# Keys of four edge chunks computed later, clearings moved on ScalarE, first gathers five slots later

## What is computed

```python
h = relu(layernorm(x))
H = gelu(h @ W1.T + b1)                       # nodes x 128
W_tar = gelu(H[src] @ WA.T) @ WB.T             # edges x 4
agg = segment_sum(H[src][:, :, None] * W_tar[:, None, :], dst)      # nodes x 128 x 4
agg = gelu(agg)
out_edge = einsum('ehm,em->eh', agg[dst], W_tar)
agg_node = segment_sum(out_edge, dst) / max(count(dst), 1)
out = gelu(concat([agg_node, H])) @ W2.T + b2
return x + out
```

## Time and profile before

| | |
|---|---|
| median of three runs | 1301.7 us (1298.65 to 1304.33) |
| the profiled execution | 1304.83 us, its span 1303.1 us |
| PE busy | 1070.4 us (82%) |
| DVE busy | 947.6 us (73%) |
| POOL busy | 903.8 us (69%) |
| ACT busy | 604.1 us (46%) |
| mean granted clock of TensorE | 0.927 |

### The profile page before, as it was taken

How to read it: one execution, slowest core, us unless ns; L and a number is a source line. 1 busy time by engine, 2 the same in 40 slices (tenths; PEclk the granted TensorE clock), 3 DMA queues, 4 the chain that set the end, 5 groups by cost and what they waited for, 6 DMA issues and landing times.

```text
span 1303.1 us, 25372 instructions
## 1 busy us (share of the span) xinstructions
PE 1070.4 (82%) x7395; PEld 727.5 (56%) x7395; DVE 947.6 (73%) x2601; ACT 604.1 (46%) x1304; POOL 903.8 (69%) x923
## 2 busy tenths in 40 slices
PE   5665127789999989999999999899999997889558
PEld 3454013356767656666666666566666654566324
DVE  7998558888888668888678887578887763532147
ACT  6765664436666445656445655356655200000224
POOL 4766657667777777777777777777777777767037
PEclk9867559989999999999999999999999998999859
DMA  5244552226666655555655555655555567655422
GB/s 206 100 161 190 227 208 56 54 76 169 181 167 175 179 156 164 156 156 156 187 164 157 157 163 159 179 151 156 155 156 152 158 197 163 201 139 161 119 76 83
DMA packets 83891, 201.11 MB, mean 154 GB/s; under 512 B 21917, under 2 KB 33375, under 8 KB 81553
## 3 DMA queue, kind: packets, MB, share of 16 engines
q1 hardware_dynamic: 58282, 142.37, 34.9%
q0 software_dynamic: 25472, 57.11, 18.1%
HBM read 167.18 MB, written 32.22 MB: 153 GB/s over the span
## 4 chain that ended last, share of the span: by engine, by line
PE 46%; DVE 17%; POOL 14%; issue 10%; DMA 7%; ACT 5%; DVEq 2%; SPq 0%; ACTq 0%; POOLq 0%
PE ps L1398 19%; POOL q L664 12%; PE ps L1379 11%; PE ps L1351 10%; DMA q<-node_table,src_g 4%; PE ps L1354 3%; DVE big L1084 2%; PE ps L1403 2%; DVE q L1093 1%; ACT hot_b L800 1%; DVE big L1280 1%; DVE mask L1059 1%; DVE big L1015 1%; DVE big L1029 1%; DVE q L948 1%
## 5 line engine op out<-in xcount | busy, mean ns | idle before, releaser
L664 POOL DMA_INDIRECT q<-node_table,src_g x796 | 770.1, 968 | 273.2 <-issue 216.6
L1398 PE MATMUL ps<-big,q 128*128 128x298 bf16 (+2 forms) x2940 | 464.0, 297 | 0.0
L800 ACT ACTIVATE hot_b<-iota_b,q 128x128 bf16<-128x128 bf16 x847 | 269.7, 389 | 343.8 <-PE ps L1379 343.6
L1351 PE MATMUL ps<-mask,q 128*128 128x96 f32 x1592 | 254.4, 283 | 76.7 <-DVE mask L1059 75.4
L1398 PEld LDWEIGHTS ps<-big,q 128*128 128x128 bf16 x2940 | 264.7, 98 | 82.7 <-issue 2.7
L1093 DVE TENSOR_SCALAR q<-iota_a,q 128x490 bf16<-128x490 f16 (+1 forms) x847 | 269.3, 365 | 24.7 <-issue 12.5
L1379 PE MATMUL ps<-q,hot_b 128*128 128x490 bf16 (+1 forms) x847 | 233.9, 372 | 58.5 <-ACT hot_b L803 25.0
L1351 PEld LDWEIGHTS ps<-mask,q 128*128 128x128 f32 x1592 | 216.7, 194 | 112.2 <-DVE mask L1059 100.7
L1084 DVE TENSOR_TENSOR big<-big,ps 128x490 f32 (+1 forms) x358 | 232.4, 649 | 55.1 <-PE ps L1379 53.8
L1059 DVE TENSOR_TENSOR mask<-eq,q 128x192 f32<-128x192 bf16 x398 | 141.5, 356 | 124.2 <-DMA q<-node_table,src_g 97.0
L1379 PEld LDWEIGHTS ps<-q,hot_b 128*128 128x128 bf16 x847 | 69.9, 97 | 161.4 <-DVE big L1084 61.4
(11 more groups left out here) (134 smaller groups left out, 776.9 us busy)
## 6 DMA issues: line engine op xcount, KB each, us to landing
q<-product_parts SPq DMA_DIRECT2D x245, 388.0 KB
product_parts<-big SPq DMA_DIRECT2D x12, 1552.0 KB, 5.9
q<-node_table,src_g POOLq DMA_INDIRECT x796
node_table<-big SPq DMA_DIRECT2D x12, 280.0 KB, 3.1
own_part<-big SPq DMA_DIRECT2D x12, 256.0 KB, 2.9
...
```

What stands on the lines that cost most here:

```text
L664: pool.indirect_dma_start(out=ring[:, t % R, :], out_offset=None, in_=table, in_offset=bass.IndirectOffsetOnAxis(ap=src_g[:, t:t + 1], axi ...
L800: last = nc.scalar.activation(hot_b[:, b % 2, i, :], iota_b[:, :], ACT.Abs, bias=nkey_b[:, t:t + 1])
L1351: nc.tensor.matmul(o[:, 0:MIX * W], ring[:, s + t, 0:D], mask[:, b, t, :, :], start=(t == 0), stop=(t == G - 1))
L1398: last = nc.tensor.matmul(ps[:, 3 + m, 0:n], c[:, LEAD + P * (MIX * part + m):LEAD + P * (MIX * part + m + 1)], counts[k % 2][:, a, c0:c1] ...
```

## The change

Keys of chunks 5 and 4 are still computed in the prologue, in steps 6 and 7. Those of chunks 3, 0, 2 and 1 are computed by DVE in the product stages: at slots 10 and 26 of stage 1, slot 26 of stage 2 and slot 26 of stage 3. Eight slots earlier SP loads the slices of destinations, sources and tile bounds that they need (three DMAs) into the memory of `stage`. The groups of chunk 0 move to stages 2 to 4. ACT's one clear of 9800 columns becomes one of 2800 in step 9 and one of 7000 in step 15; of six wipes two go to step 7 of the prologue's loop, and the other four into slots 1 to 3 of stage 0. The gathers of stage 0 begin in slot 5 and are spread over 25 slots in place of 30.

```diff
+KEYED = {K - 1: 1, K - 2: 1, K - 3: 2, 0: 3, K - 4: 4, K - 5: 5}
+KEY_AT = {(1, 2): K - 3, (1, 18): 0, (2, 18): K - 4, (3, 18): K - 5}
+KEY_LAG = 8
...
-LOW_GROUPS = [0, 14, 13, 7, 0, 0]
+LOW_GROUPS = [0, 0, 16, 14, 4, 0]
...
-        until = NT - 6 if stage == S else slots
+        late, until = (0 if stage else 5), (NT - 6 if stage == S else slots)
...
-                            [g0 + g for g in share(GATHERS[stage], q, until)],
+                            [g0 + g for g in share(GATHERS[stage], q - late, until - late)],
```

SP, after the load of the part of unit (s, a):

```diff
+                if (s, a) in KEY_AT:
+                    k = KEY_AT[s, a]
+                    dst_k, src_k, tmin_k = raw(k)[0:3]
+                    sp.wait_ge(keys_ready, KEYED[k] - 1)
+                    if s >= 2:
+                        sp.wait_ge(dense_stored, 32 * (s - 1))
+                    sp.dma_start(dst_k, dst_e[:, FROM[k]:TO[k]]).then_inc(ld_raw, 16)
+                    sp.dma_start(src_k, src_e[:, FROM[k]:TO[k]]).then_inc(ld_raw, 16)
+                    sp.dma_start(tmin_k, bounds[0:1, FROM[k]:TO[k]].to_broadcast([P, TO[k] - FROM[k]])).then_inc(ld_raw, 16)
```

ACT, in the steps of the prologue between the copy of a row (L753) and the high part (L769), then between the prologue and stage 0, then in the slots behind the hot batches:

```diff
+                if c == 7:
+                    act.wait_ge(st_bounds, 32)
+                    wipe(TAIL0 - 2 * GC, 2 * GC)
+                    wipe(t0[4], TAIL[4])
+                if c == 9:
+                    act.wait_ge(consts, 7)
+                    clear(1, FREE_ROW, NT)
                 if c == NCH + 2:
...
-                    clear(1, 0, NT)
+                    clear(1, 0, FREE_ROW)
...
-            act.wait_ge(st_bounds, 32)
-            wipe(TAIL0 - 2 * GC, 2 * GC)
-            wipe(t0[3], TAIL[3] + TAIL[4])
-            act.wait_ge(row_stored[0], 16 * ((NCH + 1) // 2))
-            act.wait_ge(row_stored[1], 16 * (NCH // 2))
-            act.wait_ge(products_made, NCH)
-            wipe(t0[2], TAIL[2])
-            for b in LAST:
-                act.wait_ge(parts_stored[b % CBUFS], 16 * (b // CBUFS + 1))
-                wipe(t0[1] + b % CBUFS * C3_WORDS, C3_WORDS)
...
+                if i == 1:
+                    act.wait_ge(row_stored[0], 16 * ((NCH + 1) // 2))
+                    act.wait_ge(row_stored[1], 16 * (NCH // 2))
+                    act.wait_ge(products_made, NCH)
+                    wipe(t0[2], TAIL[2] + TAIL[3])
+                if 1 <= i <= CBUFS:
+                    b = LAST[i - 1]
+                    act.wait_ge(parts_stored[b % CBUFS], 16 * (b // CBUFS + 1))
+                    wipe(t0[1] + b % CBUFS * C3_WORDS, C3_WORDS)
```

DVE, in the steps of the prologue, and in the slots ahead of the gathers:

```diff
-                if 6 <= c < 6 + K:
-                    chunk_keys(ORDER[c - 6])
-                if c == 6 + K:
+                if 6 <= c < 8:
+                    k = K - 1 - (c - 6)
...
+                if (s, slot.at - KEY_LAG) in KEY_AT:
+                    k = KEY_AT[s, slot.at - KEY_LAG]
+                    v.wait_ge(ld_raw, 48 * (KEYED[k] - 1))
+                    chunk_keys(k, *raw(k), keys_ready)
```

More of the change, by code:

```diff
@@ L142 @@
 KEYS = [c.key + t for slot in SLOTS for c in slot.counts for t in range(c.size)]
+CHUNK_OF = [c.chunk for slot in SLOTS for c in slot.counts for t in range(c.size)]
 BUILT = [sum(len(slot.counts) for slot in SLOTS if slot.stage < s) for s in range(S + 1)]
@@ L357, in gnn_kernel @@
         keys_ready = sem("keys_ready")
+        first_keys = sem("first_keys")
+        ld_raw = sem("ld_raw")
         z_ready = sem("z_ready")
@@ L797, in hot_batch @@
                     act.wait_ge(counted, HB * (b - 1))
+                act.wait_ge(keys_ready, max(KEYED[CHUNK_OF[HB * b + i]] for i in range(n)))
                 for i in range(n):
@@ L955, in chunk_keys @@
                 chained()
-                link(nc.vector.scalar_tensor_tensor(ka, out_of, GUARD, ka, ALU.mult, ALU.add))
+                nc.vector.scalar_tensor_tensor(ka, out_of, GUARD, ka, ALU.mult, ALU.add).then_inc(done_sem, 1)
             def gather_keys():
```

38 lines of the change are left out of this document (25 added, 13 removed).

## The result

The changed kernel takes 1318.08 us (median of 4 runs, 1316.42 to 1322.51), the kernel before, timed beside it, 1303.01 (4 runs, 1298.65 to 1308.42). The ratio is 1.0118, 95% interval 1.0093 to 1.0143: slower by 1.2%, where 1297 had been forecast and 1310 was the upper end of the range. The profiled execution took 1316.57 us, its span is 1314.8, that is 11.7 more than the span before.

A forecast was written before the change was run, and what follows sets the result against it. The limit changes by stage: DVE and POOL alternate in the prologue, DVE leads stage 0, gathers and PE the later stages. Terms -7.3 - 2.2 - 3.5 - 3 + 17 + 1.5 - 7.5 = -5.0 us gave 1299.8, predicted 1297; range 1284 to 1310.

The forecast's parts named there:

- the moved tiles: Stages 2 to 4 gain 84 tiles at 0.20 us each: 17 us lost (bounds nothing to 42).
- the key blocks: Key blocks on DVE within the stages, largely covered by PE's work in hand: 1.5 us lost (0 to 6).
- the stage boundaries: Stages 2 and 3 end with a full ring, helping the starts of stages 3 to 5: 7.5 us gained (0 to 10).
- stage 1: Loses 84 tiles and becomes purely the gather stream's, 165 of 167.9 us: 3 us gained (0 to 4).
- The prologue's keys: Four prologue steps without keys take 10.2 us each, 40.8 in place of 48.05: 7.3 us gained.
- The clear: Split in two in the prologue, so DVE's L1015 waits less behind it: 2.2 us gained (0 to 2.4).
- the wipes: Moved from before stage 0, so the first add of counts comes earlier: 3.5 us gained (bounds 9.5 and -1).
- The 4.2 us stall: In stage 0 DVE waits 4.2 us for ACT's fourth batch, which stands behind wipes and a clear.
- The rival of the dearer tiles: In stages 2 to 4 moved tiles cost 0.35 us each, DVE and PE working in turn: 1309 us; chance 0.17.
- Stage 5 and the tail: From the end of stage 4 to the kernel's end: forecast difference 0.
- The gathers held up by DVE: DVE's added 37 us in the stages stops POOL for a third of it, stream 12 us later: 1309; chance 0.03.

The follow-up runs named there:

- e2: Kernel before with only the clearings in their new places and the gathers five slots later; keys and groups as before: 1299.69 us, ratio 0.9977.
- e1: Kernel before with only the table of low groups changed, moving chunk 0's groups to stages 2 to 4; all keys in the prologue: 1327.29 us, ratio 1.0199.
- e16: Changed kernel with the old table of groups, chunk 0's keys in the prologue again and three key blocks in stage 1: 1298.96 us, ratio 0.9967.
- e3: Changed kernel with all four key blocks in stage 1, and ACT's evacuations between stages waiting for all five key signals: 1315.91 us, ratio 1.0102.
- e13: e1 with DVE's adds of chunk 0's groups made on only 6 of 49 node tiles: 1328.87 us, ratio 1.0206.
- e14: e1 with DVE's one-hots of chunk 0's tiles written on 64 columns only: 1328.79 us, ratio 1.0205.
- e4: Changed kernel with 22 unused PE passes over zeros ahead of PE's wait in slot 26 of stage 3: 1315.46 us, ratio 1.0113.
- e15: e1 with PE's passes for chunk 0's tiles made on 64 columns only: 1338.04 us, ratio 1.0276.

## Why the prediction was wrong

The sum of -5.0 became +11.7. The front held. What failed is the price of stages 1 to 4: the moved tiles at 0.20 us each (0.28 measured), the key blocks taken as covered (1.5 us; 5 to 7), and two gains that did not exist, at the stage boundaries (7.5 us) and in stage 1 (3 us). Term by term:

**The prologue's keys, -7.3: right, and small.** 9.25, at 9.7 us a step. POOL and DVE do take turns, as assumed, and a step is 0.5 us shorter than the sum of its parts had it; e2 against the changed kernel gives 9.2 at the first add.

**The clear -2.2 and the wipes -3.5: right.** Together 13.2 us at the first add in e2 and 8.1 at the first unit, where 11.5 and 5.7 had been forecast; up to 2.6 us of such a difference is the execution's. The 4.2 us stall came as 4.23.

**Stage 1, -3: wrong, +1.3.** It lost 84 tiles and did not shorten, nor did it in e1. There was nothing to gain, since the stage was the gather stream's already. POOL between the end of the first unit and the end of the stage, before and after (gathers; then idle time in us, times):

```profile
L664 POOL DMA_INDIRECT q<-node_table,src_g x129: 940/944/1121, 288.1 to 449.7; - x129
...
  issue: 35.7, 117
  PE ps L1354: 3.7, 12
```

```profile
L688 POOL DMA_INDIRECT q<-node_table,src_g x131: 940/944/1156, 270.9 to 434.5; - x131
...
  issue: 38.7, 127
  PE ps L1391: 1.2, 4
```

That is 0.30 us between two gathers in both, and 1.26 and 1.25 us a gather. The 167.9 us of the earlier trace rows hold 133 gathers, which is all of it; the forecast's 165 came from an estimate of how full the ring is at either end. The window from 260.00 to 435.10 has 140 gathers; at 1.25 us each (0.944 and 0.30) they are 175 of its 175.1 us. The forecast had this limit right, but let the stage begin with a full ring: at the end of its first unit POOL was 7 gathers ahead of PE, 9 before, of the ring's 10. In 166 to 260 only 64 gathers were made, where 94 us hold 75: the two stalls of POOL there emptied what the later start was to leave. This also says where the front's gain goes. What stage 0 saves, stage 1 waits out behind the gathers, 3.5 us in e2 and 7.6 in e16 (the latter has three key blocks there; e3, with two more than the changed kernel, took 3.1 more).

**The moved tiles, +17: wrong in size, +23.9.** This is the largest cost, and with it alone the sum would have been +1.9. The 0.20 was a slope between two stages that differ in tiles the one way and in groups the other. The rows of PE give 0.22 us a tile busy and 0.03 of waiting there, 0.26 and 0.13 (5.4 / 42) in the change, less what masks give back. The prediction had put the point from which the change is slower at 0.26 us; 0.28 was measured, so this term alone is past the turn. The rival of the dearer tiles named the right term, with 0.35 as its price; its reason, that DVE makes the turns long, is not borne out (e13, e14).

**The key blocks in stages 2 and 3, +1.5: wrong, 5 to 7.** The changed kernel's stages 2 to 4 are 6.7 us longer than e1's and 5.1 longer than e3's. The block's length was nearly right (3.25 us, 2.8 taken). The cover was wrong: "PE has up to six one-hots and a unit of matmuls in hand" looked at the counts, but PE's next instruction was the pass behind a mask, and masks stand behind the block. The second part, the drop of the clock after a wait of 2.5 us, was in no term. The block in stage 2 cost 1.8 us in its own slots (33.8 us in the changed kernel and in e4, 32.0 in e3), of which 0.7 came back in the eight behind. The length of the whole stage does not show it: 201.0, 201.1 in e3, and 203.2 in e4, which has the same blocks.

**The stage boundaries, -7.5: wrong, at most -3.** Windows around the three boundaries, before and after:

```profile
634.80:669.80 35.00, 30.13 (x220) 21.36 (x219) 19.40 (x63) 12.90 (x35) 26.46 (x29) 0.95 0.64 178
827.60:862.60 35.00, 29.70 (x219) 21.10 (x217) 17.83 (x57) 10.93 (x29) 26.47 (x29) 0.95 0.64 174
1026.60:1061.60 35.00, 32.41 (x252) 22.53 (x250) 23.73 (x48) 1.65 (x6) 26.47 (x29) 1.00 0.70 196
```

```profile
626.10:661.10 35.00, 31.48 (x237) 22.65 (x234) 20.57 (x65) 13.08 (x35) 26.47 (x29) 0.95 0.65 181
836.70:871.70 35.00, 30.50 (x226) 21.83 (x224) 19.93 (x65) 12.39 (x32) 26.03 (x28) 0.95 0.63 170
1041.40:1076.40 35.00, 33.14 (x258) 22.96 (x256) 23.78 (x48) 1.65 (x6) 26.46 (x29) 1.00 0.71 202
```

PE is busy 2.9 us more in the three, and part of that is more tiles. POOL's busy time is 26.5 us in five of the six and 26.0 in one: 28 or 29 gathers fill any such window, at their own pace. A ring that is full earlier in the stage is nearly empty again at its end, since the last three slots have no counts and PE uses ten gathers there in 8.4 us, faster than 1.25 us each. At the ends of stages 2 and 3 POOL was 5 gathers ahead of PE, 4 before; the last three units took 8.4 us, 9.2 and 9.3 before. The term is counted within stages 2 to 4, so the tiles' 23.9 us is net of it.

**Stage 5 and the tail, 0: -3.2.** The tail is 77.2 us in the changed kernel and 77.1 to 77.9 in e1, e2, e3, e13 to e15, but 80.4 in e16 and 80.1 before. But e1, whose front, stage 5 and tail are those of the kernel before, has 77.3, so this is a difference between executions and not the change's. Its cause was not looked for.

The misses add up: -4.1 (first unit) + 4.3 (stage 1) + 6.9 (tiles) + 5.2 (keys) + 7.5 (boundaries) - 3.2 (tail) = 16.6, against the 16.7 between -5.0 and +11.7. The largest single one is a gain that never existed, at the boundaries; the tiles come next. The sign of the change hangs on tiles and keys: take both back (e16), and it is faster.

**The gathers held up by DVE: not seen.** The gather's own length stayed as it was, 0.951 us in stage 3 (145.48 / 153) beside a DVE with 168.59 us busy, 0.947 in stage 5 (120.26 / 127) beside 76.00. The Trainium skill, page SBUF — State Buffer, section "Who interferes with whom", states that VectorE in one of its two-port modes contends with GpSimd, and that the one that issued second stands still meanwhile. No trace here shows this for gathers; in which mode VectorE's one-hots ran, no run here shows.

What stays open: how the 0.28 us divides between PE's pass (0.22 or 0.26 by its busy time, in the two comparisons above) and the handovers of a group and of a batch, and why it is 0.3 in stages 2 and 3 and 0.22 in stage 4. Relief of one engine at a time gave nothing; whether that is because three engines stand close behind one another, or because of the clock, the runs don't tell.
